# One core, 2048 rows of a bilinear tower: GpSimd waits for the landing of the four gathers ahead of the last four

## The reference

```
e = jnp.stack([tbl_0[ids[:, 0]], ..., tbl_39[ids[:, 39]]], axis=1)      # (2048, 40, 64)
p = inputs[:, rowidx]                                                     # 780 pairs, first field
q = inputs[:, colidx]                                                     # second field
out = jnp.einsum('bie,fie,bif->bi', p, param, q)                          # z, (2048, 780)
h = jnp.concatenate([z, dense_ctx], axis=1)
h = jnp.maximum(h @ W_top1 + b_top1, 0.0)
h = jnp.maximum(h @ W_top2 + b_top2, 0.0)
y = h @ W_top3
```

## Time and profile before

| | us |
|---|---|
| median of 3 runs | 1275.88 (1272.23 to 1280.07) |
| profiled execution, its time | 1274.63 |
| its span, first to last instruction | 1272.8 |
| mean granted TensorE clock | 0.993 |
| busy in the span: PE, DVE, ACT, POOL | 1231.0, 1023.4, 1023.9, 577.7 |

### The profile page before, as it was taken

The page is one execution under the profiler, slowest core; times in us unless marked ns, Lnnn a source line. Parts: engine busy times, 40 slices in busy tenths (PEclk is TensorE's granted clock), DMA queues, the critical chain, the costliest instruction groups (busy, mean ns, idle before and its releaser), DMA issues.

```text
span 1272.8 us, 23705 instructions
## 1 busy us (share of the span) xinstructions
PE 1231.0 (97%) x6064; PEld 481.1 (38%) x6064; DVE 1023.4 (80%) x1680; ACT 1023.9 (80%) x7945; POOL 577.7 (45%) x615
## 2 busy tenths in 40 slices
PE   6788999999999999999999999999999999999999
PEld 3233433333333343333344333433343333343333
DVE  5768999998887777888787887788889787788980
ACT  0049988777488989998958999899968898999981
POOL 5555555555555555555345555555225554000000
PEclk9989999999999999999999999999999999999999
DMA  6311422132221222222221222122112122111100
GB/s 173 94 46 46 143 72 70 45 94 64 71 70 48 70 71 70 49 67 64 66 67 47 73 69 71 45 70 72 54 59 69 46 70 67 30 47 50 44 2 0
DMA packets 33201, 80.88 MB, mean 64 GB/s; under 512 B 11773, under 2 KB 12285, under 8 KB 32937
## 3 DMA queue, kind: packets, MB, share of 16 engines
q1 hardware_dynamic: 12320, 57.17, 13.9%
q0 software_dynamic: 19456, 19.96, 7.7%
q10 hardware_dynamic: 1288, 2.24, 0.6%
HBM read 79.32 MB, written 0.01 MB: 62 GB/s over the span
## 4 chain that ended last, share of the span: by engine, by line
PE 60%; ACT 31%; issue 3%; DMA 2%; POOL 2%; DVE 1%; another core or an unknown queue 1%; ACTq 0%
ACT wide_prod L541 29%; PE ring L727 26%; PE z_ps L750 13%; PE ring L732 11%; PE ring L756 7%; DMA rows<-tbl,idx_now 2%; POOL rows L481 2%; PE ring L701 2%; ACT e_t L502 1%; PE ring L760 1%; DMA idx_now<-idx 0%; DVE prod L606 0%; PE ring L763 0%; PE ring L708 0%
## 5 line engine op out<-in xcount | busy, mean ns | idle before, releaser
L541 ACT ACTIVATE wide_prod<-wide_prod 128x64 f32<-128x64 f32 x3904 | 933.7, 243 | 52.4 <-DVE wide_prod L619 25.6
L481 POOL DMA_INDIRECT rows<-tbl,idx_now x608 | 576.9, 949 | 496.7 <-DMA rows<-tbl,idx_now 292.2
L541 ACT ACTIVATION_READ_ACCUMULATOR wide_prod<-wide_prod 128x1 f32 x3904 | 739.4, 189 | 24.4 <-issue 23.4
L606 DVE TENSOR_TENSOR prod<-ring,e_t 128x512 f32<-128x512 f32 x1008 | 630.8, 683 | 147.6 <-PE ring L727 101.1
L727 PE MATMUL ring<-e_t,w 64*128 64x512 f32 x2176 | 563.0, 609 | 9.6 <-ACT e_t L502 5.9
L619 DVE TENSOR_TENSOR wide_prod<-ring,rows 128x512 f32<-128x512 f32 x512 | 328.3, 682 | 44.6 <-PE ring L732 33.3
L727 PEld LDWEIGHTS ring<-e_t,w 64*128 64x128 f32 x2176 | 215.9, 187 | 300.1 <-issue 203.7
L732 PE MATMUL ring<-w,e_t 64*128 64x512 f32 x1024 | 292.1, 607 | 11.4 <-ACT e_t L502 7.1
L750 PE MATMUL z_ps<-prod,strip 128*32 128x512 f32 x2096 | 256.2, 603 | 0.1
L732 PEld LDWEIGHTS ring<-w,e_t 64*128 64x128 f32 x1024 | 106.2, 186 | 147.0 <-issue 86.7
L750 PEld LDWEIGHTS z_ps<-prod,strip 128*32 128x32 f32 x2096 | 55.3, 109 | 182.0 <-issue 119.6
(11 more groups left out here) (23 smaller groups left out, 79.3 us busy)
## 6 DMA issues: line engine op xcount, KB each, us to landing
w<-weights SPq DMA_DIRECT2D x64, 768.0 KB
rows<-tbl,idx_now POOLq DMA_INDIRECT x608
w<-weights SPq DMA_DIRECT2D x4, 512.0 KB
z_t<-tbl SPq DMA_DIRECT2D x8, 224.0 KB
w<-w1z SPq DMA_DIRECT2D x1, 1792.0 KB
h<-hot_ids ACTq DMA_DIRECT2D x6, 256.0 KB
z_t<-hot_ids ACTq DMA_DIRECT2D x2, 256.0 KB
w<-w2p SPq DMA_DIRECT2D x1, 512.0 KB
```

The costliest lines, as they stand in the source:

```text
L481: nc.gpsimd.indirect_dma_start(out=rows[:, slot, t, E * f:E * f + E], out_offset=None, in_=tables[m * 2 + f], in_offset=bass.IndirectOffse ...
L541: last = nc.scalar.activation(products, products, ACT.Copy, accum_out=z_b[:, h, t, col:col + 1])
L606: nc.vector.tensor_tensor(dst[:, j, :], ring[:, bank, :], e_t[:, k, :], ALU.mult).then_inc(t_free, 1)
```

## The change

The wait behind each four gathers is no longer for those four, but for the four before them, in all of the run and across tiles. So four gathers may be under way while the next four are issued. For that each place in `rows` gets two semaphores, one for each field, and TensorE waits for both before it transposes a tile: one wait more for each of the 76 gathered tiles. Nothing else is moved: the gathers, their order, their sizes and all other engines' instructions stay.

```diff
-        gathered = [sem(f"gathered{i}") for i in range(2 * FIXED + G_SLOTS)]
+        gathered = [[sem(f"gathered{i}_{f}") for f in range(2)] for i in range(2 * FIXED + G_SLOTS)]
...
             pool.wait_ge(idx_in, 16)
+            under_way = None
             for tile in GATHERED:
...
-                        ).then_inc(gathered[slot], 16)
-                    if c > 0 or m > 0 or f > 0:
-
-                        pool.wait_ge(gathered[slot], 16 * BT * (f + 1 + 2 * (use - 1)))
+                        ).then_inc(gathered[slot][f], 16)
+                    if under_way is not None:
+
+                        pool.wait_ge(*under_way)
+                    under_way = gathered[slot][f], 16 * BT * use
...
             def transpose_tile(tile):
                 slot, use = slot_of(tile)
-                pe.wait_ge(gathered[slot], use * 2 * BT * 16)
+                for f in range(2):
+                    pe.wait_ge(gathered[slot][f], use * BT * 16)
```

## The result

At its first timing the changed kernel took **1799.53 us** (median of 6 runs, 1790.16 to 1807.14), the kernel before 1274.82 beside it: a ratio of 1.4106, 95% interval 1.4074 to 1.4139. The forecast was 1265.0 with a range of 1260 to 1271, so it was wrong by 534.5 us, and in direction.

A forecast was written before the change was run, and what follows sets the result against it. The prediction took TensorE's chain to be bound at the start by its wait for tile 3's gathers: 7.80 us of wait plus 3.13 of clock make 10.93, from a median of 1275.88 to 1265.0 us, range 1260 to 1271.

The forecast's parts named there:

- the last sentence on what is added: Later waits for landings, some 240 us, give nothing; a denser stream of gathers meets DMA engines 0.10 busy outside the loads.
- VectorE's comparisons: Comparisons may slow as GpSimd works in 16.7 us of former waits: taken as 0, upper end 7.3 us.
- The start: TensorE's wait for tile 3's gathered rows goes wholly, 7.80 us; at the late end 0.9 of it stays.
- the term of 3.13 us: Tile 3's transpositions, sixteen sums and four matmuls at full instead of half clock: 0.46 + 1.72 + 0.95 us back.
- ScalarE's first sum: Sign of being right: it starts at 80.2 - 10.9 = 69.3 us.
- The gathers of tiles 0 to 3: Ninth gather at about 18.8 us, 1.42 us each beside comparisons, the 32nd off GpSimd at 51.2 and landed at 52.7.
- The added waits on TensorE: One more wait for each of 76 tiles: taken as 0, upper end 3.0 us.
- Rival 4: Slower: each added TensorE wait stops its queue for 0.30 us, 22.8 us in all, giving 1287.8 us; chance 0.03.
- GpSimd held by transpositions in place of landings: Sign of being right: GpSimd is held much longer by transpositions, where it had waited for landings.
- Rival 1: GpSimd is held longer beside VectorE's comparisons, 1.62 us a gather; tile 3 lands 1.2 us late: 1266 to 1269; chance 0.14.
- Shift reaches the end: Work after 65.67 us is in fixed order and moves along, so the whole shift is taken as gain.

The follow-up runs named there:

- A: Occasion of the first timing, called delayed: kernel before 1274.8 us, changed kernel at a ratio of 1.411.
- C: Later occasion, called delayed: kernel before 1273.0 us, changed kernel at 1.409, other kernels at 1.361 to 1.399.
- D: Later occasion, called delayed: kernel before 1260.6 us, changed kernel at 1.405, other kernels at 1.000, 1.001 and 1.298.
- B: Later occasion, called quiet: kernel before 1246.7 us, other kernels at 0.985 to 0.999; the changed kernel was not run.
- E: Later occasion, called quiet: kernel before 1248.0 us, other kernels at 0.982, 0.982 and 1.028; the changed kernel was not run.
- F: Later occasion, called quiet: kernel before 1242.7 us, changed kernel at 0.985, other kernels at 0.985 and 0.989.
- experiment 2: Changed kernel with a GpSimd memset of 128 x 1700 bytes behind each four gathers, keeping the pace of before: 0.9929 on B, 1.0014 on D.
- split-semaphore kernel: Changed kernel with its two semaphores a place, but GpSimd waits for its own four gathers as before: 1242.99 us against 1246.73, ratio 0.9994.
- experiment 1: Changed kernel, but GpSimd waits behind its own four gathers as before: 1242.99 us against 1246.73 on B, ratio 0.9994.
- the steady 1.42 us: Changed kernel with a memset of 128 x 830 bytes behind each four gathers, an even 1.42 us a gather: 0.9823 on E, 0.9889 on F.

## Why the prediction was wrong, point by point

**The step that failed** is the last sentence on what is added: "a denser stream of gathers meets engines that are 0.10 busy outside the loads". It priced the denser stream by the share of the DMA engines alone, at zero. The runs put the price of a dense stream at 510 to 525 us on A, C and D and at nothing on B, E and F. In no rival did the gathers hurt other engines, and the one term that has GpSimd slow another engine, VectorE's comparisons, was put at 0 with an upper end of 7.3 us. That GpSimd's pace is the cause on delayed occasions is shown by experiment 2 (same waits, pace of before: 1.0014 beside 1.4048). What it brings is shown by the trace of A: TensorE's semaphore updates reach VectorE up to 54 us late and ScalarE 8.9 us late, and ScalarE's own instructions start late. Why that follows from the pace, and why only on some occasions, stays open. The opening says that the engines meet only at semaphores; the gaps between ScalarE's sums suggest that here they also meet somewhere else.

**A sign stood in the trace of before and was not read:** these two lines of its waits.
```profile
ACT wide_prod L541 <- issue: 46.8, 100, 1.0
...
ACT e_t L502 <- remote: 3.7, 1, 3.7
```
ScalarE's sums need nothing from each other, yet stopped a hundred times. Neither line is there in the split-semaphore kernel on B, the equal of the kernel before. The "issue" line tells the occasions apart without an exception: it is in all ten traces from A, C and D, those at a pace of 1.60 us included, and in none of the ten from B, E and F. So the kernel before may already have been paying on A: 1260.6 to 1274.8 us on the delayed occasions against 1242.7 to 1248.0 on the quiet ones, 1 to 2.6%. That its own gathers are what costs this is not shown. The lines say that something disturbs; they could not have told 41%.

**The start went as forecast where nothing is delayed.** Timeline of TensorE in the changed kernel on F, 46 to 80 us:
```profile
56.22 1.99 PE L730 MATMUL ring<-e_t,w 64*128 64x512 f32 x8 [0.69 <-ACT e_t L504]
58.13 0.66 PE L704 MATMUL ring<-ident,rows 128*128 128x128 f32 x4
59.48 1.13 PE L730 MATMUL ring<-e_t,w 64*128 64x512 f32 x4 [0.69 <-ACT e_t L504]
60.54 1.92 PE L753 MATMUL z_ps<-prod,strip 128*32 128x512 f32 x16
...
67.02 3.70 PE L735 MATMUL ring<-w,e_t 64*128 64x512 f32 x16
```
and the same stage with the old pace on B (split semaphores):
```profile
64.45 1.09 PE L702 MATMUL ring<-ident,rows 128*128 128x128 f32 x4 [7.19 <-issue]
...
68.23 3.64 PE L751 MATMUL z_ps<-prod,strip 128*32 128x512 f32 x16
...
76.45 3.70 PE L733 MATMUL ring<-w,e_t 64*128 64x512 f32 x16
```
Tile 3 is transposed at 58.13 us (forecast 57.9) without a wait. Its four transpositions, four matmuls and sixteen sums took 0.66, 1.13 and 1.92 us, the full-clock times that the term of 3.13 us was made of the earlier trace rows. The first wide comes 9.4 us earlier (76.45 - 67.02), and ScalarE's first sum stands at 69.50 us (forecast 69.3):
```profile
69.50 0.26 ACT L543 ACTIVATE wide_prod<-wide_prod 128x64 f32<-128x64 f32 x1 [10.08 <-DVE wide_prod L621]
```
- *The gathers of tiles 0 to 3* were earlier than counted. The 32nd started at 43.81 us on A and left GpSimd at 44.76, not 51.2: the first four had landed by the time the eighth was issued (the ninth started at 16.09, not at 18.8), and the 26 gathers from 10 to 44 us took 1.031 us each on A, not 1.116. The sum had tile 3 in time even at 51.2, so this changed nothing in it. Even on A GpSimd waited for a landing only 0.3 us in the whole run.
- *The added waits on TensorE:* taken as 0, right (experiment 1; experiment 2 on D). Rival 4 is refuted, though its sign came true by another way.
- *GpSimd held by transpositions in place of landings:* right, 239.8 us in 19 waits on F.
- *Rival 1, comparisons hold the gathers.* The trace shows the opposite in the delayed stretches: the gathers keep their 1.25 us and the comparisons come late. The Trainium skill ("SBUF — State Buffer", Who interferes with whom) has a `tensor_scalar` in a two-port mode and an instruction of GpSimd exclude each other for a whole instruction. That is no account of this: the comparisons shown last 0.49 to 0.63 us, it is their release that is late, and ScalarE is late too.
- *Shift reaches the end:* right on F, with more to come. The median fell by 17.5 us (1242.66 to 1225.18), where 10.9 was forecast. A second wait for gathers lies later. The trace of before on A doesn't have it, perhaps because TensorE came there later and GpSimd was ahead. The split-semaphore kernel on B, 340 to 375 us:
```profile
354.16 0.66 PE L702 MATMUL ring<-ident,rows 128*128 128x128 f32 x4
360.58 1.09 PE L702 MATMUL ring<-ident,rows 128*128 128x128 f32 x4 [5.76 <-issue]
361.60 3.79 PE L728 MATMUL ring<-e_t,w 64*128 64x512 f32 x8
...
370.79 1.88 PE L728 MATMUL ring<-e_t,w 64*128 64x512 f32 x8
```
TensorE sat 5.76 us before the second of two tiles (with two semaphores to wait for, the profile names no releaser, here as at 64.45 us). Behind it the clock was down (0.55 granted from 360.5 to 366 us): 0.43 us on the transpositions (1.09 - 0.66) and 1.91 on the eight matmuls (3.79 - 1.88), 8.1 in all. With 10.3 at the start (7.19 and 3.1 of clock) that makes 18.4; the spans of the two, from two quiet occasions, differ by 16.9 (1240.6 - 1223.7).

**Other versions.** On quiet occasions the change, waits behind every eight and the steady 1.42 us lie at 0.982 to 0.989; nothing beat that. Of those run on both kinds two are not measurably slower on either: the paused kernel of experiment 2 (0.9929 and 1.0014) and the changed waits for tiles 0 to 3 alone (0.9908 and 0.9999). On D the paused kernel's runs lie at 1258.30 to 1267.71 us, as close together as those of the kernel before, while the other's lie at 1251.07 to 1281.86. Since the 1.5% can turn into a loss of 41%, the paused kernel is the safe choice, for 0.7% on a quiet occasion and nothing on a delayed one.

**Still open:** what makes an occasion delayed (not the chip: D and F shared it; the code was the same); by what path the gathers hold up TensorE's updates and ScalarE's instructions; whether pace, unbroken length, or rows gathered per us decides.

## What to carry to other kernels

A wait that looks like idle time of an engine off the critical path may be pacing it; before it is taken away, ask not only who waits for that engine but what its instructions do to the others at the higher rate. Gaps without a releaser between instructions that need nothing of each other, and "remote" waits in a kernel on one core, came here in every trace of a delayed occasion and in none of a quiet one; where they are seen, price the change with such a coupling as a rival. Where a wait names no releaser, work out from the code which instruction should have ended it, and when that one was done. Time a change that makes a queue denser on more than one occasion, with its control beside it each time.

## What the hardware showed that was not expected

- On a delayed occasion (A), GpSimd's indirect gathers 1.25 us apart went with semaphore updates of TensorE reaching VectorE 5.60 us apart and up to 54 us late, some of them still late 10 us after the last gather, and with gaps of up to 1.9 us between ScalarE's instructions without semaphores, while the DMA engines were 0.14 busy. At 1.60 us apart (on D): ratio 1.0014.
- The same code on the same chip took 1770.42 us on D and 1225.18 on F (ratios 1.4048 and 0.9846), while the kernel before moved by 1.4% (1260.55 and 1242.66).
- A gather's time on GpSimd hardly depends on its rows: 0.91 us for 64, 0.95 for 128.
